# A router's matmuls turned round: weights stationary, all tokens moving, and the logits transposed back inside the next block

## The chip, the cores and the metric

The kernel runs on one core of a Trainium2 chip. The metric is the device time of one execution in microseconds, as the median of several runs; the kernel before takes 953.7 us.

## The reference

The input is x, 384 tokens by 1024 features, fp32. The first layer is graph attention (layer norm, q, k, v projections and their second projections, 16 heads, a mask built from 6144 edges, an output projection, added to x). The second is switch attention, and the change lies in its first step:

```python
def _get_sel_gate(x, w, route_scale):
    logits = jnp.einsum('bsd,ed->bse', x, w).astype(jnp.float32)
    raw = logits.reshape(x.shape[0], x.shape[1], H, E)
    probs = jax.nn.sigmoid(raw)
    vals, idx = jax.lax.top_k(probs, K)
    vals = vals / jnp.clip(vals.sum(-1, keepdims=True), 1e-09)
    vals = vals * route_scale
    gate = (jax.nn.one_hot(idx, E, dtype=vals.dtype) * vals[..., None]).sum(-2)
    return gate
gate_v = _get_sel_gate(x, sel_v_w, rs)
gate_o = _get_sel_gate(x, sel_o_w, rs)
```

Here x is the layer-normed sum after the first layer, H = 8 heads, E = 8 experts, K = 2. The 64 + 64 rows of sel_v_w and sel_o_w are one block of 128 router outputs. The gates weigh the experts' values and outputs of each head (v = sum over experts of gate_v times x @ v_w; out = sum of gate_o times context @ o_w), between which lies ordinary attention with q and k.

## The kernel before, in words

Weights come from HBM as 201 units of 128 x 1024 fp32 (512 KB), through a ring of three slots. SyncE issues a load for a slot once its low part is made (line 247). ScalarE copies the unit to fp32r, the high part (`hi_fixed`, lines 340 to 345, and `hi_at`, 330 to 338), after the unit two earlier has been used. GpSimd subtracts (`make_lo`, line 277) and gives the low part. TensorE then works a unit with three matmuls for each product, high by high, high by low, low by high (`three`, lines 994 to 998).

Two sorts of unit matter. In a column unit (`column_unit`, lines 1005 to 1011) a 128 x 128 block of the weights is stationary and the 384 tokens of the transposed activations hT move: 8 steps of three matmuls of 384 columns; the result has outputs on the partitions and tokens along the row. In a row unit (`row_unit`) a block of activations is stationary and 512 columns of weights move.

Between the two layers the order is this. The last output projection finishes token tile after token tile (t = 0, 1, 2). VectorE adds each to x (line 793) and makes its statistics; GpSimd makes 1/sqrt (lines 269, 272); ScalarE normalises into `normed` (line 350); TensorE transposes 8 blocks (`normed_turns`, lines 1045 to 1055, by `turn`, line 1043); ScalarE copies each half to hT_hi (`hT_his`, line 357); VectorE subtracts to hT_lo (`hT_los`, line 595).

The router (lines 1160 to 1177) is the unit U_ROUTER. Before the change it has the activations stationary and 128 columns of weights moving, for each tile by itself: 24 matmuls of 128 columns for tile 0, then the transposes of tile 2, then 24 for tile 1 and 24 for tile 2. Its result has tokens on the partitions, as the gates need it. When all are done, ScalarE takes the exponential of the logits (line 464), and VectorE runs a chain of small instructions, each waiting for the one before (lines 822 to 858): sigmoid, two largest of eight, their weights, the gates (line 857). ScalarE's order by hand is: normalise 0, normalise 1, hT_his 0, normalise 2, hT_his 1, weight copy U_ROUTER + 1, hT_his 2, weight copy U_ROUTER + 2, the exponential, further weight copies.

On TensorE the router is followed by head 0's q unit (U_HEAD, bank 5) and k unit, three of the four value units of the first four experts, three transposes of the gates (which wait for `gates_ready`), the fourth value unit, the scores, and from there the heads' loop without a change. The value units begin only after `router_exp`, since they write bank 2, which holds the logits. `normed` and the start of the logits' new place (`logits_T`) are the same piece of `scratch`, columns 3072 on; it is free once tile 0's transposes are done.

Of the kernel before, what the change touches and what calls it, by code (L numbers as in the profile page):

```python
# [14 lines left out]
P = 128  # L15
N = 384
NT = N // P
D = 1024
KT = D // P
# [13 lines left out]
RING = 3  # L33
U_PAIR = 3 * PAIRS
U_WO = U_PAIR + 3 * PAIRS
U_ROUTER = U_WO + 8
U_HEAD = U_ROUTER + 1
# [9 lines left out]
LN_STEPS = 2 * NT  # L47
RF = 2
GF = 7
QF, KF = 5, 0  # L50
# [33 lines left out]
def gnn_switch_kernel(nc, x_in, units, biases, bo, edge_type_weights, route_scale, edge_cols, src_row, dst_row, out):  # L84
    fp32, f32r, bf16 = mybir.dt.float32, mybir.dt.float32r, mybir.dt.bfloat16
    fp16, int32 = mybir.dt.float16, mybir.dt.int32
    ALU, ACT, AX = mybir.AluOpType, mybir.ActivationFunctionType, mybir.AxisListType.X

    ctx = ExitStack()
    with ctx:  # L90
        def sb(name, shape, dt):
            return ctx.enter_context(nc.sbuf_tensor(name, shape, dt))

        def sem(name):
            return ctx.enter_context(nc.semaphore(name))
# [3 lines left out]
        w_hi = sb("w_hi", [P, RING, D], f32r)  # L99
        w_lo = sb("w_lo", [P, RING, D], f32r)  # L100

        hT_hi, hT_lo = sb("hT_hi", [P, KT, N], f32r), sb("hT_lo", [P, KT, N], f32r)
# [14 lines left out]
        scratch = sb("scratch", [P, 6144], fp32)  # L117
# [47 lines left out]
        bank = [ctx.enter_context(nc.psum_tensor(f"bank{i}", [P, 512], fp32)) for i in range(8)]  # L165
# [6 lines left out]
        hi_ready, unit_used = sem("hi_ready"), sem("unit_used")  # L172
        lo_ready = [sem(f"lo_ready{s}") for s in range(RING)]
# [5 lines left out]
        normed_T, hT_hi_done, hT_lo_done = sem("normed_T"), sem("hT_hi_done"), sem("hT_lo_done")  # L179
# [23 lines left out]
        v_gated, fv_hi_done, fv_lo_done = sem("v_gated"), sem("fv_hi_done"), sem("fv_lo_done")  # L203
        f_scores, f_max, f_exp, f_norm = sem("f_scores"), sem("f_max"), sem("f_exp"), sem("f_norm")
        f_probs_T, f_pT_hi, f_pT_lo = sem("f_probs_T"), sem("f_pT_hi"), sem("f_pT_lo")
        f_context, context_ready = sem("f_context"), sem("context_ready")
        gated_ready, gc_hi_done, gc_lo_done, out_added = (sem("gated_ready"), sem("gc_hi_done"), sem("gc_lo_done"),
                                                          sem("out_added"))
# [1 line left out]


        bo_row = mask8[:].rearrange("p t n -> p (t n)")[:, 0:D]

        x_tiles = x_in.rearrange("(t p) d -> p t d", p=P)
        out_tiles = out.rearrange("(t p) d -> p t d", p=P)
# [106 lines left out]
        def _(act):  # L322
# [17 lines left out]
            def hi_fixed(u, fresh=False):  # L340
                s = u % RING
                act.wait_ge(raw_landed[s], 16 * (u // RING + 1))
                if not fresh:
                    act.wait_ge(unit_used, u - (RING - 1))
                act.activation(w_hi[:, s, :], w_raw[:, s, :], ACT.Copy).then_inc(hi_ready, 1)

            def normalise(turn, t):

                act.wait_ge(rstd_ready, turn * NT + t + 1)
                act.activation(normed[:, t, :], x[:, t, :], ACT.Identity, scale=rstd[:, t:t + 1],  # L350
                               bias=shift[:, t:t + 1]).then_inc(normed_ready, 1)

            def hT_his(turn, t):
                for f in range(2):
                    n = 2 * t + f
                    act.wait_ge(normed_T, turn * LN_STEPS + n + 1)
                    act.activation(hT_hi[:, 4 * f:4 * f + 4, t * P:(t + 1) * P],
                                   bank[LN_BANKS[n]][:].rearrange("p (k n) -> p k n", k=4),
                                   ACT.Copy).then_inc(hT_hi_done, 1)
# [93 lines left out]
            for u in range(U_WO + 5, U_ROUTER + 1):  # L453
# [3 lines left out]
            hT_his(1, 0)  # L457
            normalise(1, 2)
            hT_his(1, 1)
            hi_fixed(U_ROUTER + 1)  # L460
            hT_his(1, 2)
            hi_fixed(U_ROUTER + 2)
            act.wait_ge(unit_used, U_ROUTER + 1)
            act.activation(route[:, 0].rearrange("p g e -> p (g e)"), bank[RF][:, 0:N], ACT.Exp,
                           scale=-1.0).then_inc(router_exp, 1)

# [526 lines left out]
        def _(pe):  # L993
            def three(dst, a_hi, a_lo, b_hi, b_lo, first, last):

                pe.matmul(dst, a_hi, b_hi, start=first, stop=False)  # L996
                pe.matmul(dst, a_hi, b_lo, start=False, stop=False)  # L997
                return pe.matmul(dst, a_lo, b_hi, start=False, stop=last)  # L998

            def unit_ready(turns, u):  # L1000

                pe.wait_ge(lo_ready[u % RING], turns + (u // RING + 1))
                return u % RING

            def column_unit(turns, u, dst, b_hi, b_lo):
                s = unit_ready(turns, u)
                for k in range(KT):
                    c = slice(k * P, (k + 1) * P)
                    last = three(dst[:, 0:N], w_hi[:, s, c], w_lo[:, s, c], b_hi[:, k, :], b_lo[:, k, :], k == 0,
                                 k == KT - 1)  # L1010
                last.then_inc(unit_used, 1)
# [30 lines left out]
            def turn(dst, src):  # L1042
                return pe.transpose(dst, src, ident[:])  # L1043

            def normed_turns(turns, t):
                if turns == 0 and t == NT - 1:
                    pe.wait_ge(last_normed, 1)
                else:
                    pe.wait_ge(normed_ready, turns * (NT - 1) + t + 1)
                for f in range(2):  # L1050
                    n = 2 * t + f
                    for kk in range(4):
                        k = 4 * f + kk
                        last = turn(bank[LN_BANKS[n]][:, kk * P:(kk + 1) * P], normed[:, t, k * P:(k + 1) * P])
                    last.then_inc(normed_T, 1)
# [7 lines left out]
            for i in range(3):  # L1063
                column_unit(0, i, bank[i], hT_hi, hT_lo)
            with pe.Fori(1, PAIRS) as j:
                for i in range(3):
                    pe.wait_ge(qkv_lo_done, j * 3 + (i - 2))
                    column_unit(j, i, bank[i], hT_hi, hT_lo)
# [40 lines left out]

            pe.wait_ge(qkv_lo_done, PAIRS * 3 - 2)  # L1110
            column_unit(0, U_PAIR, bank[6], qT_hi, qT_lo)
            pe.wait_ge(qkv_lo_done, PAIRS * 3 - 1)
            column_unit(0, U_PAIR + 1, bank[0], kT_hi, kT_lo)
# [34 lines left out]
            for t in range(NT):  # L1148
                tok = slice(t * P, (t + 1) * P)
                for k in range(4, KT):  # L1150
                    s = s_7 if k > 5 else s_6
                    c = slice(k % 2 * HALF, (k % 2 + 1) * HALF)
                    last = three(bank[WO_BANKS[1][t]][:, 0:HALF], oT_hi[:, k, tok], oT_lo[:, k, tok], w_hi[:, s, c],
                                 w_lo[:, s, c], False, k == KT - 1)
# [2 lines left out]
                last.then_inc(unit_used if t == NT - 1 else tile_done, 1)  # L1157


            def router(t):  # L1160
                pe.wait_ge(hT_lo_done, LN_STEPS + 2 * t + 2)
                tok = slice(t * P, (t + 1) * P)
                for k in range(KT):
                    c = slice(k * P, (k + 1) * P)
                    s = U_ROUTER % RING
                    last = three(bank[RF][:, tok], hT_hi[:, k, tok], hT_lo[:, k, tok], w_hi[:, s, c], w_lo[:, s, c],
                                 k == 0, k == KT - 1)
                return last

            normed_turns(1, 0)  # L1170
            normed_turns(1, 1)
            pe.wait_ge(lo_ready[U_ROUTER % RING], U_ROUTER // RING + 1)
            pe.wait_ge(out_added, 2 * NT)
            router(0)
            normed_turns(1, 2)
            router(1)
            router(2).then_inc(unit_used, 1)


            def values_units(head, g, turns, u, experts=range(4), third=None):  # L1180
# [33 lines left out]
                    row_unit(turns, u + i, OF[f], gc_hi, gc_lo, i,  # L1214
                             (out_added, head * 6 + 7) if f else None)

            column_unit(0, U_HEAD, bank[QF], hT_hi, hT_lo)
            column_unit(0, U_HEAD + 1, bank[KF], hT_hi, hT_lo)
            pe.wait_ge(router_exp, 1)
            values_units(0, 0, 0, U_HEAD + 2, range(3))  # L1220
# [1 line left out]
            for t in range(NT):  # L1222
                last = turn(bank[GF][0:FH * FE, t * P:(t + 1) * P], gates[:, t, FH * FE:2 * FH * FE])
# [40 lines left out]
            for n in range(8):  # L1264
                f, i = n // 4, n % 4
                u = U_LAST + n
# [68 lines left out]
```

## Time and profile before

| | |
|---|---|
| median of 3 runs | 953.7 us (953.54 to 954.23) |
| the profiled execution | 953.67 us |
| its span, first to last instruction | 951.9 us |
| TensorE matmul busy | 934.1 us |
| VectorE, ScalarE, GpSimd busy | 484.0, 370.9, 512.9 us |
| HBM traffic | 130 MB, 137 GB/s over the span |

The span is 1.8 us shorter than the execution's own time, for what lies around the instructions. Busy times of TensorE are overlaps of pipelined matmuls, so the distance from start to start tells a matmul's price, not its duration. "PE" in the rows is TensorE, "DVE" VectorE, "ACT" ScalarE, "POOL" GpSimd. Times in the rows are us from the start of the span.

### The profile page before, as it was taken

What the parts mean: (1) busy time and instruction counts of PE and PEld (TensorE: products, weight loads), DVE (VectorE), ACT (ScalarE), POOL (GpSimd) and SP (SyncE); (2) the same over time, 40 slices, a digit from 0 to 9 for tenths busy, and PEclk for the clock granted to TensorE, in tenths of its full rate; (3) what the DMA queues carried; (4) which work ended last, traced back from release to release, by engine and by line L of the source; (5) the groups of instructions that cost most, each with busy time, mean ns of one, the idle gap of its engine ahead of it and who ended that gap; (6) DMA issues with size and microseconds to landing.
All of it is one profiled execution on the core that took longest, in us unless ns stands there. A gap on an engine that the chain in (4) does not pass through costs nothing.

```text
span 951.9 us, 14149 instructions
## 1 busy us (share of the span) xinstructions
PE 934.1 (98%) x4779; PEld 830.4 (87%) x4779; DVE 484.0 (51%) x1065; ACT 370.9 (39%) x593; POOL 512.9 (54%) x265
## 2 busy tenths in 40 slices
PE   5999999999999999999999999999999999999998
PEld 4999999999988879888888888888888888888887
DVE  7988855565652683812731642362182264154361
ACT  4333355455642423423433332343243243243331
POOL 4677763434335455565555555565556546556553
PEclk9999999999999999999999999999999999999999
DMA  7656643221223245443443353354353335335332
GB/s 277 183 187 185 183 134 105 75 86 66 88 82 104 80 136 178 177 133 113 149 158 132 103 198 118 132 174 134 117 184 118 132 120 185 113 111 199 133 111 89
DMA packets 38134, 130.43 MB, mean 137 GB/s; under 512 B 5920, under 2 KB 7648, under 8 KB 37088
## 3 DMA queue, kind: packets, MB, share of 16 engines
q1 hardware_dynamic: 31632, 110.25, 34.0%
q10 hardware_dynamic: 4944, 19.86, 6.5%
q0 software_dynamic: 1536, 0.03, 0.1%
q8 instruction: 14, 0.23, 0.1%
q14 instruction: 8, 0.07, 0.0%
HBM read 127.83 MB, written 2.29 MB: 137 GB/s over the span
## 4 chain that ended last, share of the span: by engine, by line
PE 83%; DMA 5%; DVE 4%; issue 4%; POOL 3%; ACT 1%; POOLq 0%; SPq 0%; DVEq 0%; ACTq 0%
PE bank L996 26%; PE bank L998 26%; PE bank L997 26%; DMA mask_scratch<-weight,cell 3%; POOL mask_scratch L281 3%; PE bank L1043 3%; PE bank L1080 1%; DMA x<-in_x 1%; DVE scratch L650 1%; DMA mask<-mask_scratch 0%; DVE scratch L832 0%; DVE scratch L836 0%; ACT scratch L417 0%; DVE scratch L855 0%; DVE scratch L825 0%
## 5 line engine op out<-in xcount | busy, mean ns | idle before, releaser
L277 POOL TENSOR_TENSOR w_lo<-w_raw,w_hi 128x1024 fp32r<-128x1024 f32 x184 | 449.4, 2446 | 388.8 <-ACT w_hi L338 317.6
L338 ACT ACTIVATE w_hi<-w_raw 128x1024 fp32r<-128x1024 f32 x166 | 175.5, 1058 | 211.4 <-PE bank L998 210.8
L996 PE MATMUL bank<-w_hi,hT_hi 128*128 128x512 f32 (+1 forms) x456 | 175.0, 384 | 0.8 <-DVE hT_lo L595 0.8
L998 PE MATMUL bank<-w_hi,hT_lo 128*128 128x512 f32 (+1 forms) x456 | 175.1, 384 | 0.0
L997 PE MATMUL bank<-w_lo,hT_hi 128*128 128x512 f32 (+1 forms) x456 | 175.0, 384 | 0.0
L996 PE MATMUL bank<-w_hi,qT_hi 128*128 128x512 f32 x384 | 150.1, 391 | 0.0
L998 PE MATMUL bank<-w_hi,qT_lo 128*128 128x512 f32 x384 | 149.5, 389 | 0.0
L997 PE MATMUL bank<-w_lo,qT_hi 128*128 128x512 f32 x384 | 149.4, 389 | 0.0
L934 DVE TENSOR_TENSOR x<-bank,x 128x512 f32<-128x512 f32 x48 | 30.4, 684 | 184.4 <-PE bank L998 184.4
L996 PE MATMUL bank<-hT_hi,w_hi 128*128 128x384 f32 x320 | 107.8, 337 | 1.5 <-DVE hT_lo L595 1.5
L997 PE MATMUL bank<-hT_lo,w_hi 128*128 128x384 f32 x320 | 107.5, 336 | 0.0
L998 PE MATMUL bank<-hT_hi,w_lo 128*128 128x384 f32 x320 | 107.5, 336 | 0.0
L996 PEld LDWEIGHTS bank<-w_hi,hT_hi 128*128 128x128 f32 x456 | 85.7, 188 | 17.4 <-issue 1.0
L998 PEld LDWEIGHTS bank<-w_hi,hT_lo 128*128 128x128 f32 x456 | 85.7, 188 | 17.0
L997 PEld LDWEIGHTS bank<-w_lo,hT_hi 128*128 128x128 f32 x456 | 85.7, 188 | 16.4
L880 DVE SCALAR_TENSOR_TENSOR scratch<-bank,v_gate,scratch 128x128 f32<-128x128 f32 x168 | 53.1, 348 | 80.7 <-PE bank L998 77.4
L998 PEld LDWEIGHTS bank<-w_hi,qT_lo 128*128 128x128 f32 x384 | 72.1, 188 | 15.1
L997 PEld LDWEIGHTS bank<-w_lo,qT_hi 128*128 128x128 f32 x384 | 72.1, 188 | 14.8
L996 PEld LDWEIGHTS bank<-w_hi,qT_hi 128*128 128x128 f32 x384 | 72.1, 188 | 14.6
L919 DVE TENSOR_TENSOR scratch<-scratch 128x384 f32<-128x384 f32 x64 | 63.8, 1006 | 16.4 <-ACT scratch L489 14.7
L281 POOL DMA_INDIRECT mask_scratch<-weight,cell x48 | 54.7, 1141 | 26.0 <-issue 13.8
L996 PEld LDWEIGHTS bank<-hT_hi,w_hi 128*128 128x128 f32 x320 | 60.6, 189 | 2.1 <-DVE hT_lo L595 1.9
(155 smaller groups left out, 1278.0 us busy)
## 6 DMA issues: line engine op xcount, KB each, us to landing
w_raw<-in_units SPq DMA_DIRECT2D x201, 512.0 KB, 3.3
scratch<-gate_rows_scratch ACTq DMA_DIRECT2D x8, 1536.0 KB, 7.3
scratch<-in_src_row ACTq DMA_DIRECT2D x8, 384.0 KB, 4.2
scratch<-in_dst_row ACTq DMA_DIRECT2D x8, 384.0 KB, 5.3
out_x<-x SPq DMA_DIRECT2D x6, 256.0 KB, 2.1
x<-in_x SPq DMA_DIRECT2D x2, 512.0 KB, 6.8
mask_scratch<-weight,cell POOLq DMA_INDIRECT x48
mask<-mask_scratch ACTq DMA_DIRECT2D x1, 576.0 KB, 3.9
```

Source lines behind the costliest of these rows:

```text
L277: pool.tensor_tensor(w_lo[:, s, :], w_raw[:, s, :], w_hi[:, s, :].bitcast(fp32), ALU.subtract).then_inc(lo_ready[s], 1)
L281: pool.indirect_dma_start(out=mask_dram, out_offset=bass.IndirectOffsetOnAxis(ap=cells, axis=0), in_=values, in_offset=None, bounds_check= ...
L338: act.activation(w_hi[:, s, :], w_raw[:, s, :], ACT.Copy).then_inc(hi_ready, 1)
L650: step.add(dve.scalar_tensor_tensor(same[:, start:start + wide], keys[:, c * P:PIECE * P], key[:, bass.ds(at, 1)], later[:, 0:wide], ALU.i ...
L880: ins = dve.scalar_tensor_tensor(v_sum[:, t, :], src, col, v_sum[:, t, :], ALU.mult, ALU.add)
L919: dve.tensor_tensor(gated[:, e % 2, :], context, gate_rows[:, e, :], ALU.mult).then_inc(gated_ready, 1)
L934: dve.tensor_tensor(x[:, t, f * HALF:(f + 1) * HALF], bank[banks[t]][:, 0:HALF], x[:, t, f * HALF:(f + 1) * HALF], ALU.add).then_inc(out_a ...
L996: pe.matmul(dst, a_hi, b_hi, start=first, stop=False)
L997: pe.matmul(dst, a_hi, b_lo, start=False, stop=False)
L998: return pe.matmul(dst, a_lo, b_hi, start=False, stop=last)
L1043: return pe.transpose(dst, src, ident[:])
L1080: last = pe.matmul(bank[NT * head + t][:, 0:N], a[p, tok], b[p, :], start=n == 0, stop=n == 2)
```

## The change

Four things: the router becomes one column unit with its weights stationary and all 384 tokens moving, after all three tiles are transposed and split; ScalarE copies its result from bank 2 to SBUF; three transposes turn it back into bank 2, and they stand on TensorE after the second of eight steps of head 0's q unit; and ScalarE makes hT_his of tile 2 before the weight copy U_ROUTER + 1, not after. The exponential waits for the transposes.

```diff
@@ declarations
+        logits_ready, logits_back = sem("logits_ready"), sem("logits_back")
+        logits_T = scratch[:, 3072:3072 + N]
@@ ScalarE
             normalise(1, 2)
             hT_his(1, 1)
+            hT_his(1, 2)
             hi_fixed(U_ROUTER + 1)
-            hT_his(1, 2)
             hi_fixed(U_ROUTER + 2)
             act.wait_ge(unit_used, U_ROUTER + 1)
+            act.activation(logits_T, bank[RF][:, 0:N], ACT.Copy).then_inc(logits_ready, 1)
+            act.wait_ge(logits_back, 1)
             act.activation(route[:, 0].rearrange("p g e -> p (g e)"), bank[RF][:, 0:N], ACT.Exp,
                            scale=-1.0).then_inc(router_exp, 1)
@@ TensorE
-            def column_unit(turns, u, dst, b_hi, b_lo):
+            def column_unit(turns, u, dst, b_hi, b_lo, between=None):
                 s = unit_ready(turns, u)
                 for k in range(KT):
+                    if between and k == 2:
+                        between()
                     c = slice(k * P, (k + 1) * P)
                     last = three(dst[:, 0:N], w_hi[:, s, c], w_lo[:, s, c], b_hi[:, k, :], b_lo[:, k, :], k == 0,
                                  k == KT - 1)
@@ TensorE
-            def router(t):
-                pe.wait_ge(hT_lo_done, LN_STEPS + 2 * t + 2)
-                tok = slice(t * P, (t + 1) * P)
-                for k in range(KT):
-                    c = slice(k * P, (k + 1) * P)
-                    s = U_ROUTER % RING
-                    last = three(bank[RF][:, tok], hT_hi[:, k, tok], hT_lo[:, k, tok], w_hi[:, s, c], w_lo[:, s, c],
-                                 k == 0, k == KT - 1)
-                return last
-
-            normed_turns(1, 0)
-            normed_turns(1, 1)
-            pe.wait_ge(lo_ready[U_ROUTER % RING], U_ROUTER // RING + 1)
-            pe.wait_ge(out_added, 2 * NT)
-            router(0)
-            normed_turns(1, 2)
-            router(1)
-            router(2).then_inc(unit_used, 1)
+            def router():
+                pe.wait_ge(hT_lo_done, 2 * LN_STEPS)
+                pe.wait_ge(out_added, 2 * NT)
+                column_unit(0, U_ROUTER, bank[RF], hT_hi, hT_lo)
+
+            def logit_turns():
+                pe.wait_ge(logits_ready, 1)
+                for t in range(NT):
+                    last = turn(bank[RF][:, t * P:(t + 1) * P], logits_T[:, t * P:(t + 1) * P])
+                last.then_inc(logits_back, 1)
+
+            for t in range(NT):
+                normed_turns(1, t)
+            router()
@@ TensorE
-            column_unit(0, U_HEAD, bank[QF], hT_hi, hT_lo)
+            column_unit(0, U_HEAD, bank[QF], hT_hi, hT_lo, logit_turns)
```

## Rows read from the trace of the kernel before

**Rows 1.** The page: busy time of each engine, and the chain by engine.
```profile
PE 934.1 (98%) x4779; PEld 830.4 (87%) x4779; DVE 484.0 (51%) x1065; ACT 370.9 (39%) x593; POOL 512.9 (54%) x265
PE 83%; DMA 5%; DVE 4%; issue 4%; POOL 3%; ACT 1%; POOLq 0%; SPq 0%; DVEq 0%; ACTq 0%
```

**Rows 2.** Groups by line, TensorE's matmuls, 315.1 to 324.07: busy, mean ns, idle before.
```profile
L996 PE MATMUL bank<-w_hi,hT_hi 128*128 128x128 f32 x24 | 6.6, 277 | 0.8 <-DVE hT_lo L595 0.8
```

**Rows 3.** Timeline of TensorE: start, duration, idle before and what ended it.
```profile
311.66 1.04 PE L1043 MATMUL bank<-ident,scratch 128*128 128x128 f32 x8
...
315.17 0.30 PE L996 MATMUL bank<-w_hi,hT_hi 128*128 128x128 f32 x1 [0.80 <-DVE hT_lo L595]
...
317.87 1.06 PE L1043 MATMUL bank<-ident,scratch 128*128 128x128 f32 x8
318.69 0.30 PE L996 MATMUL bank<-w_hi,hT_hi 128*128 128x128 f32 x1
...
323.97 0.28 PE L998 MATMUL bank<-w_hi,hT_lo 128*128 128x128 f32 x1
324.08 0.39 PE L996 MATMUL bank<-hT_hi,w_hi 128*128 128x384 f32 x1
...
328.31 0.33 PE L996 MATMUL bank<-hT_hi,w_hi 128*128 128x384 f32 x1
...
344.53 0.39 PE L998 MATMUL bank<-w_hi,hT_lo 128*128 128x512 f32 x1
345.75 0.52 PE L1043 MATMUL bank<-ident,mask 128*64 128x128 f32 x3 [0.84 <-DVE mask L857]
```

**Rows 4.** Timeline of ScalarE around the router.
```profile
314.70 1.24 ACT L350 ACTIVATE scratch<-x,shift,rstd 128x1024 f32<-128x1024 f32 x1 [0.51 <-POOL shift L272]
...
316.80 1.06 ACT L345 ACTIVATE w_hi<-w_raw 128x1024 fp32r<-128x1024 f32 x1
318.53 1.09 ACT L357 ACTIVATE hT_hi<-bank 128x512 fp32r<-128x512 f32 x2 [0.67 <-PE bank L1043]
...
324.28 0.49 ACT L464 ACTIVATE scratch<-bank 128x384 f32<-128x384 f32 x1 [3.72 <-PE bank L998]
...
328.57 1.06 ACT L345 ACTIVATE w_hi<-w_raw 128x1024 fp32r<-128x1024 f32 x1 [2.85 <-PE bank L998]
```

**Rows 5.** Timeline of VectorE: the splits of hT, and three of the gates' chain.
```profile
313.74 1.29 DVE L595 TENSOR_TENSOR hT_lo<-bank,hT_hi 128x512 fp32r<-128x512 f32 x2
316.46 1.29 DVE L595 TENSOR_TENSOR hT_lo<-bank,hT_hi 128x512 fp32r<-128x512 f32 x2 [1.44 <-ACT hT_hi L357]
319.16 1.29 DVE L595 TENSOR_TENSOR hT_lo<-bank,hT_hi 128x512 fp32r<-128x512 f32 x2 [1.42 <-ACT hT_hi L357]
...
341.21 0.21 DVE L849 TENSOR_TENSOR best<-best 128x48 f32<-128x48 f32 x1
...
342.36 2.75 DVE L855 TENSOR_TENSOR scratch<-scratch,best 128x384 f32<-128x384 f32 x1
345.14 0.56 DVE L857 TENSOR_TENSOR mask<-scratch 128x384 f32<-128x384 f32 x1
```

**Rows 6.** Timeline of GpSimd: two of its weight subtractions.
```profile
342.07 2.62 POOL L277 TENSOR_TENSOR w_lo<-w_raw,w_hi 128x1024 fp32r<-128x1024 f32 x1 [1.67 <-ACT w_hi L345]
346.15 2.40 POOL L277 TENSOR_TENSOR w_lo<-w_raw,w_hi 128x1024 fp32r<-128x1024 f32 x1 [1.46 <-ACT w_hi L345]
```

**Rows 7.** Timeline of TensorE at the start.
```profile
12.09 3.68 PE L1043 MATMUL bank<-ident,scratch 128*128 128x128 f32 x16 [0.64 <-ACT scratch L350]
17.23 0.69 PE L996 MATMUL bank<-hT_hi,w_hi 128*128 128x384 f32 x1 [1.46 <-DVE hT_lo L595]
...
20.23 0.33 PE L996 MATMUL bank<-hT_hi,w_hi 128*128 128x384 f32 x1
```

**Rows 8.** Windows, start-up: length, busy of PE, PEld, DVE, ACT, POOL, clock, DMA, GB/s.
```profile
10.00:20.00 10.00, 7.90 (x32) 7.10 (x31) 8.66 (x15) 8.60 (x12) 5.42 (x6) 1.00 0.90 322
```

## The prediction, made before the changed kernel was run

> **What bounds the kernel now.** I read the page first. TensorE is busy in 98% of the span and holds 83% of the chain that ended last [rows 1], so a change pays only where it shortens TensorE's own stream or a wait in it. Then the groups of TensorE's instructions in the router's stretch: 72 matmuls and 8 transposes fill 8.9 us (315.17 to 324.08), 24 of each of three kinds as in the row, with a wait of 0.8 us ahead of them [rows 2, 3]. The matmuls move 128 columns and start 0.111 us apart: (323.97 - 318.69) / 47 = 0.112. The next block, head 0's q with 384 columns moving, takes 24 matmuls from 324.08 to 328.31, 4.23 us, or 0.176 each [rows 3]. So the same arithmetic costs about half with the weights stationary.
>
> Then TensorE's order of time after the router: it has issued all it may at 344.76 (344.53 and the 0.23 by which 512-column matmuls follow each other) and begins again at 345.75, released by VectorE's line 857, the last of the gates [rows 3]. This wait decides the case. What sets the end at 345.75 is a chain and not TensorE: router ends, ScalarE's exponential at 324.28 [rows 4], VectorE's top-two work to the end of line 857 at 345.70 (345.14 + 0.56) [rows 5]. TensorE has 1.0 us to spare against it. Afterwards TensorE runs without a wait to the end of the span, so the change is worth what line 857 is moved by, and no more.
>
> **The sum, part by part.**
>
> (1) *When all tokens are ready.* The router now starts once, after tile 2's last hT_lo. ScalarE's normalise of tile 2 is not moved: 314.70 + 1.24 = 315.94 [rows 4]. Its transposes no longer stand behind the first router tile, so they start at about 316.0, not 317.87. Four of them let ScalarE copy after 318.53 - 317.87 = 0.66 us, at 316.65. ScalarE is busy with tile 1's copies until 316.80, the moment at which it now takes the weight copy; the moved hT copies take that place: 316.80, not 318.53. VectorE starts its subtraction 0.63 us after ScalarE (319.16 - 318.53), which would be 317.43, but tile 1's pair holds it until 316.46 + 1.29 = 317.75. The pair ends at 319.04 [rows 5]. TensorE followed such a pair by 0.14 (315.17 - (313.74 + 1.29)) [rows 3, 5]. Router start: **319.18**, 4.0 us later than now.
>
> (2) *The router.* 24 matmuls as in head 0's q: 4.23 us, end of issue 323.41, against 324.08: 0.67 us earlier. Half the work is gone (8.0 us of matmuls become 4.2), but most of that goes into waiting for tile 2.
>
> (3) *The way back.* The exponential now starts 0.31 us after the last router matmul starts (324.28 - 323.97), that matmul being 0.28 long; with one of 0.33 ScalarE's copy starts at 323.24 + 0.33 + 0.04 = 323.61. Its length is that of the exponential of the same shape, 0.49 [rows 4]: 324.10. TensorE meanwhile has six matmuls of head 0's q, 6 x 0.176 = 1.06 us, until 324.47; they cover the copy with 0.4 us to spare, and without them TensorE would stand for the 0.7 us itself. The transposes' spacing is that of the eight between 317.87 and 318.69, 0.10 to 0.11 [rows 3]: three are 0.33 us. The last starts at about 324.7, ends 0.28 later, and the exponential starts at **325.05**, 0.77 us later than 324.28.
>
> (4) *VectorE's chain.* At its present length it would end at 345.70 + 0.77 = 346.47. But its length depends on GpSimd. Line 855 takes 2.75 us (342.36 to 345.11), line 857, with the same shapes, 0.56 [rows 5]; line 855 ends 0.42 after GpSimd's subtraction of 342.07 + 2.62 = 344.69 [rows 6]. Four instructions of the chain with both inputs in SBUF are held so (2.3 to 2.8 us each). GpSimd's schedule follows TensorE's blocks, which move by -0.67 + 0.33 = -0.34 us, while VectorE moves by +0.77. I replayed the chain with the rule that whichever of the two starts first holds the other; with today's times it gives 345.68. With the shifts the last hold falls on line 849 (now 341.21, between two subtractions): GpSimd's instruction runs 341.73 to 344.13, and then lines 849 to 857 follow unhindered, 0.06 + 0.27 + 3 x 0.56 with gaps, 2.1 us: 346.25. **Line 857 ends 0.5 us later.** If the shifts differ by 0.1 less, the replay passes through another order and gives 0.05; with no help from the holds it is 0.8. These are the ends.
>
> (5) *TensorE's side.* It would reach the gates' transposes at 344.76 - 0.34 = 344.4, so its wait grows from 1.0 us to 1.8. The 4 us of matmuls saved are gone: 3.4 of them waiting for tile 2, the rest in this wait.
>
> (6) *What is moved on other queues.* On ScalarE the weight copy of head 0's q goes behind the two hT copies: 317.9 instead of 316.80; GpSimd's part then runs 319.1 to 321.5, needed at 323.41: 1.9 us of cover. The next weight copy ends by 320.1, its GpSimd part by 323.9, needed at 328.0. The load into the first slot starts 1.1 us later and has until 328 (ScalarE's copy at 328.57 [rows 4]), over 6 us. ScalarE now also stands at the wait for the transposes; behind it is the weight copy for the first values block, which moves from 324.67 to 325.4, its GpSimd part ready near 329.0 and needed at 332.2. All free; without the 1.9 us of cover a slip would go into the router's end one for one.
>
> Sum: +0.5 us for everything behind the gates. The profiled execution took 953.67 us (its span 951.9 and 1.8 around it), so 954.17; it stands 0.03 under the median of 953.70, and I forecast **954.2 us**. A measurement of this kernel can tell about 0.2%, 1.9 us, from no change; this is inside it.
>
> **Clock.** In the start-up stretch transposes ran from 12.09 for 3.68 us, 0.23 us each, and the ten matmuls from 17.23 to 20.23 still started 0.33 us apart on the mean: 384 columns in that time are the level of 1.2 GHz, and the 0.176 later that of 2.4 [rows 3, 7]. The granted clock of that stretch nevertheless reads 1.00 [rows 8], so I go by spacing. Around the router the spacing shows no fall now: TensorE has transposes and two short waits from 311.66 to 315.17, 3.5 us, and then starts fast [rows 3]. With the change the stretch without matmuls lasts until 319.18, 7.5 us, with 24 transposes (some 2.7 us) in it.
> The Trainium skill, TensorE: Matmul & The Clock Gate, "What's actually happening", lets the clock fall to 1.2 GHz after idleness, and "Part 4: PE-mode transpose" says that transposes do not count as busy in the same way. By these the router would start slow and the sum would be rival A's. The trace agrees in so far as transposes did not lift the clock at the start [rows 7]; it shows no fall.
>
> **Rivals.**
>
> *A, slower: the clock falls before the router.* Place: the 7.5 us just named; it decides if transposes do not keep the clock up. Price: at the start the nine spacings from 17.23 to 20.23 took 3.00 us, where 9 x 0.176 are 1.58: 1.4 us lost before the clock rose. If all 24 router matmuls ran slow, 24 x (0.32 - 0.176) = 3.5 us. It falls fully on the gates' chain. I take 2.1, nearer the only rise that is seen: 956.3 (955.6 to 957.7). For it: a stretch twice the present one, and the start-up transposes. Against: the present 3.5 us without matmuls did nothing, and the stretch is not idle.
>
> *B, slower: one more hold.* Line 857 starts now at 345.14, GpSimd's next subtraction at 346.15 [rows 5, 6]. If that one comes first, line 857 is held for its 2.4 us: 956.6. The replay puts line 857 ahead, though in (4) by only 0.1 us, and behind once the shifts of the two differ by 1.6 us and not 1.1. The Trainium skill, SBUF — State Buffer, "Who interferes with whom", gives the port to the one that starts first, for its whole instruction; the row at 342.36 agrees.
>
> *C, faster: the gates' chain gives way.* Had it no weight at all, TensorE could gain its present wait of 1.0 us and the 0.3 of (5): 1.3 us: 952.4. That is still inside 0.2%. Only an error in several terms at once makes it faster by more.
>
> *D, the change does not do what it says:* the router's matmuls do not get their 0.176 because their weights are freshly made and start late. Then it ends by up to 1 us later: 955.2, inside the bound too.
>
> **The numbers.** Forecast 0.50, its own range 953.3 to 955.2 (the ends of (4) and a few tenths between executions, with D above); C 0.03 and D 0.05, both inside the bound; A 0.35, of which 0.02 falls under the bound; B 0.05; faster by several errors at once 0.02. So same 0.50 + 0.03 + 0.05 + 0.02 = 0.60, slower by over 0.2% (above 955.6) 0.33 + 0.05 = 0.38, faster (below 951.8) 0.02. The range 953.3 to 957.1 leaves out the top of A and a little below, under 2 in 10.
>
> **What would show it.** Right: router matmuls from about 319.2, 0.174 apart; the copy near 323.6; three transposes after the sixth matmul of head 0's q with no gap; the exponential near 325.0; the wait at line 857 grown to about 1.8 us; everything after it shifted by 0.5. Wrong: router matmuls 0.32 apart (A), a 2.4 us line 857 (B), a gap inside head 0's q, or a wait at the gates under 1 us.

## The result and the profile after

The changed kernel takes 955.79 us in the median of 22 runs (953.97 to 957.42), the kernel before 954.12 us in 22 runs of its own. The ratio is 1.0016, 95% interval 1.0008 to 1.0023: about 1.5 us slower, inside the 0.2% that I had called no change. The profiled execution took 955.83 us, its span 954.1.

The page of the changed kernel, busy time of each engine, beside [rows 1]:

```profile
PE 932.1 (98%) x4734; PEld 828.0 (87%) x4734; DVE 483.9 (51%) x1065; ACT 371.6 (39%) x594; POOL 512.5 (54%) x265
```

TensorE does 2 us less and the end comes later. Its timeline around the router answers to [rows 3]:

```profile
310.93 1.04 PE L1050 MATMUL bank<-ident,scratch 128*128 128x128 f32 x8
312.55 1.09 PE L1050 MATMUL bank<-ident,scratch 128*128 128x128 f32 x8 [0.58 <-ACT scratch L353]
315.27 1.09 PE L1050 MATMUL bank<-ident,scratch 128*128 128x128 f32 x8 [1.62 <-ACT scratch L353]
318.27 0.69 PE L1001 MATMUL bank<-hT_hi,w_hi 128*128 128x384 f32 x1 [1.91 <-DVE hT_lo L600]
318.75 0.53 PE L1002 MATMUL bank<-hT_lo,w_hi 128*128 128x384 f32 x1
319.07 0.53 PE L1003 MATMUL bank<-hT_hi,w_lo 128*128 128x384 f32 x1
...
324.08 0.34 PE L1001 MATMUL bank<-hT_hi,w_hi 128*128 128x384 f32 x1
324.25 0.34 PE L1002 MATMUL bank<-hT_lo,w_hi 128*128 128x384 f32 x1
...
326.17 0.49 PE L1050 MATMUL bank<-ident,scratch 128*128 128x128 f32 x3
...
347.98 0.52 PE L1050 MATMUL bank<-ident,mask 128*64 128x128 f32 x3 [1.75 <-DVE mask L862]
```

The router's matmuls start 0.32 us apart until 324, then 0.17. So until 324 TensorE is at the lower level. Here the granted clock shows it too. Windows of the changed kernel: length, busy of PE, PEld, DVE, ACT, POOL, clock, DMA, GB/s:

```profile
316.00:317.00 1.00, 0.36 (x4) 0.12 (x2) 1.00 (x3) 1.00 (x3) 0.00 (x0) 1.00 0.07 16
317.00:318.00 1.00, 0.00 (x0) 0.00 (x0) 1.00 (x3) 1.00 (x3) 0.00 (x0) 0.54 0.00 0
318.00:323.00 5.00, 4.73 (x15) 4.73 (x16) 0.21 (x1) 1.05 (x2) 4.70 (x2) 0.50 0.20 68
323.00:324.00 1.00, 1.00 (x5) 1.00 (x4) 0.00 (x0) 0.00 (x0) 0.00 (x0) 0.55 0.46 184
324.00:325.00 1.00, 1.00 (x8) 1.00 (x7) 0.00 (x0) 0.00 (x0) 0.00 (x0) 1.00 0.99 283
```

It falls to one half, 1.2 GHz, just after 317, in the wait for hT_lo ahead of the router, and is back at 324. So this execution is rival A of the prediction.

ScalarE has the copy and the exponential [rows 4]:

```profile
325.32 0.49 ACT L467 ACTIVATE scratch<-bank 128x384 f32<-128x384 f32 x1 [6.27 <-PE bank L1003]
326.69 0.49 ACT L469 ACTIVATE scratch<-bank 128x384 f32<-128x384 f32 x1 [0.88 <-PE bank L1050]
```

**A measure for the stretch.** In the traces of this case this part begins between 310.2 and 313.1 us, so I do not compare clock times of two traces but the distance from the first transposes of tile 0 (row 310.93 here, 311.66 in [rows 3]) to the transposes of the gates, which end TensorE's wait. Before: 345.75 - 311.66 = 34.09 us. Changed: 347.98 - 310.93 = 37.05 us, 2.96 more. Below it is called the stretch. What follows it is the same in every trace that has the gates' transposes in this place: the execution's time less 347.98, the end of the stretch, is 607.85 us in the changed kernel, 607.92 before, and between 607.79 and 608.14 in all ten such traces. So the kernels differ in the stretch alone, and a good part of the spread between executions of one kernel comes from when the stretch begins.

### The profile page after: what moved, and what is told of

Read it like the earlier page. It is cut to its first block, busy times and chain, and to the rows that moved or that the text cites. A ratio compares the mean times of both kernels' runs of the same rounds, so it can differ in the third digit from the quotient of the medians.

```text
span 954.1 us, 14060 instructions
## 1 busy us (share of the span) xinstructions
PE 932.1 (98%) x4734; PEld 828.0 (87%) x4734; DVE 483.9 (51%) x1065; ACT 371.6 (39%) x594; POOL 512.5 (54%) x265
## 4 chain that ended last, share of the span: by engine, by line
PE 83%; DVE 4%; DMA 4%; issue 4%; POOL 4%; ACT 1%; POOLq 0%; SPq 0%; DVEq 0%; ACTq 0%
PE bank L1001 26%; PE bank L1003 26%; PE bank L1002 26%; DMA mask_scratch<-weight,cell 3%; POOL mask_scratch L284 3%; PE bank L1050 3%; PE bank L1087 1%; DVE scratch L655 1%; DMA x<-in_x 1%; DMA mask<-mask_scratch 0%; DVE scratch L837 0%; DVE scratch L844 0%; ACT scratch L420 0%; DVE scratch L841 0%; DVE stats L586 0%
## 5 line engine op out<-in xcount | busy, mean ns | idle before, releaser
L1003 PE MATMUL bank<-w_hi,hT_lo 128*128 128x512 f32 x432 | 168.5, 390 | 0.0
L1002 PE MATMUL bank<-w_lo,hT_hi 128*128 128x512 f32 x432 | 168.4, 390 | 0.0
L1001 PE MATMUL bank<-w_hi,hT_hi 128*128 128x512 f32 x432 | 168.3, 390 | 0.0
L1001 PE MATMUL bank<-hT_hi,w_hi 128*128 128x384 f32 x328 | 111.2, 339 | 3.4 <-DVE hT_lo L600 3.4
L1002 PE MATMUL bank<-hT_lo,w_hi 128*128 128x384 f32 x328 | 110.7, 338 | 0.0
L1003 PE MATMUL bank<-hT_hi,w_lo 128*128 128x384 f32 x328 | 110.6, 337 | 0.0
L1003 PEld LDWEIGHTS bank<-w_hi,hT_lo 128*128 128x128 f32 x432 | 81.1, 188 | 17.0
L1002 PEld LDWEIGHTS bank<-w_lo,hT_hi 128*128 128x128 f32 x432 | 81.1, 188 | 16.4
L1001 PEld LDWEIGHTS bank<-w_hi,hT_hi 128*128 128x128 f32 x432 | 81.1, 188 | 16.3
```

## The experiments

All were timed against the kernel before on the same chip: e1 to e4 on one, e5 to e8 on a second, e9 to e12 on a third. Mean granted clocks are of single executions; one without a recorded fall reads 1.00. The fall of 3.4 us in e9's trace makes it 0.998, that of nearly 7 us in the changed kernel's 0.996.

**e1, unread matmuls in the idle time.**

```diff
-            for t in range(NT):
-                normed_turns(1, t)
+            def fill(n):
+                for _ in range(n):
+                    pe.matmul(bank[1][:, 0:N], k2_hi[:, 0:P], q2_hi[:], start=True, stop=True)
+
+            normed_turns(1, 0)
+            normed_turns(1, 1)
+            pe.wait_ge(out_added, 2 * NT)
+            fill(8)
+            normed_turns(1, 2)
+            fill(9)
             router()
```

> The changed kernel with 8 matmuls that nothing reads (384 columns, bank 1) between the transposes of tile 1 and tile 2 and 9 more between those of tile 2 and the router, in time in which TensorE stood. Theory (the stretch without matmuls lets the clock fall, and that is the loss): granted clock 1.00 throughout, router matmuls 0.17 to 0.18 us apart, the exponential 2.5 to 3 us earlier against the last projection matmul than in the changed kernel, time 0.3 to 0.8 us above the kernel before. Rival (the loss is the wait for tile 2 and the way back, the clock only goes along): time as the changed kernel, 1.5 to 2 us above the kernel before.

Measured: ratio 0.9996 (0.9985 to 1.0007), granted clock 1.00 in all of 12 executions. TensorE's timeline:

```profile
311.65 1.04 PE L1050 MATMUL bank<-ident,scratch 128*128 128x128 f32 x8
...
314.11 1.64 PE L1180 MATMUL bank<-q_hi,k_hi 128*128 128x384 f32 x8
315.99 1.09 PE L1050 MATMUL bank<-ident,scratch 128*128 128x128 f32 x8 [0.24 <-ACT scratch L353]
316.84 1.84 PE L1180 MATMUL bank<-q_hi,k_hi 128*128 128x384 f32 x9
318.99 0.45 PE L1001 MATMUL bank<-hT_hi,w_hi 128*128 128x384 f32 x1 [0.31 <-DVE hT_lo L600]
...
324.32 0.49 PE L1050 MATMUL bank<-ident,scratch 128*128 128x128 f32 x3
346.13 0.52 PE L1050 MATMUL bank<-ident,mask 128*64 128x128 f32 x3 [1.75 <-DVE mask L862]
```

Adding 17 matmuls that nothing reads makes the changed kernel faster: its ratio goes from 1.0016 to 0.9996. The stretch is 346.13 - 311.65 = 34.48 us: 2.57 under the changed kernel and 0.39 over the kernel before. So in these traces the fall costs 2.57 us, and everything else that the change does costs 0.39. The time expected, 0.3 to 0.8 us above the kernel before, did not show in the median, which is 0.4 below by the ratio; e9 gives the reason.

**e2, transposes in place of these matmuls** (12 and 14 of `pe.transpose(bank[1][:, 0:P], ident[:], ident[:])`).

> The changed kernel with 12 and 14 transposes of 128 columns in the same two places, in place of matmuls. If only matmuls keep the clock up: it falls to 0.50 near 317 in the profiled execution or in most of the others, time 1.5 to 2.5 us above the kernel before. If any work of TensorE keeps it up (it is idleness that lets it fall): clock 1.00, time 0.3 to 0.8 us above.

Measured: ratio 0.9994 (0.9983 to 1.0006), 11 of 12 executions at 1.00; the stretch is 344.74 - 310.28 = 34.46 us, as in e1. These transposes keep the clock up as the matmuls do.

```profile
312.83 1.47 PE L1180 MATMUL bank<-ident 128*128 128x128 f32 x12
314.62 1.09 PE L1050 MATMUL bank<-ident,scratch 128*128 128x128 f32 x8 [0.32 <-ACT scratch L353]
315.55 1.69 PE L1180 MATMUL bank<-ident 128*128 128x128 f32 x14
317.62 0.45 PE L1001 MATMUL bank<-hT_hi,w_hi 128*128 128x384 f32 x1 [0.38 <-DVE hT_lo L600]
```

From 311.9 to 317.6 there are only transposes here, and the router still starts at the upper level. What let the clock fall in the changed kernel was the idle time between, not the kind of work.

**e3, e1 without the way back.** It leaves out the turning of the logits, so its gates are others. The cuts against e1:

```diff
-            act.activation(logits_T, bank[RF][:, 0:N], ACT.Copy).then_inc(logits_ready, 1)
-            act.wait_ge(logits_back, 1)
...
-            column_unit(0, U_HEAD, bank[QF], hT_hi, hT_lo, logit_turns)
+            column_unit(0, U_HEAD, bank[QF], hT_hi, hT_lo)
```

> As e1, but without ScalarE's copy and the three transposes; the exponential reads the router's result as it is, outputs on the partitions. It leaves out the turning of the logits, so the gates are others. My sum prices the way back at 1.44 us of the exponential's start (0.49 copy, 0.4 standing behind q's matmuls, 0.33 transposes and latencies). Theory: exponential 1.4 us earlier than in e1, and line 862 earlier by 0.5 to 1.9 as the holds by GpSimd fall; time 0.2 to 0.8 us below the kernel before, since TensorE then waits less at the gates. If the way back is hidden: as e1.

Measured: ratio 0.9980 (0.9967 to 0.9992), 1.9 us less, where 0.2 to 0.8 was expected. The exponential, first in e1, then in e3:

```profile
324.85 0.49 ACT L469 ACTIVATE scratch<-bank 128x384 f32<-128x384 f32 x1 [0.88 <-PE bank L1050]
...
324.02 0.49 ACT L467 ACTIVATE scratch<-bank 128x384 f32<-128x384 f32 x1 [3.69 <-PE bank L1001]
```

In e1 the exponential starts 324.85 - 311.65 = 13.20 us into the stretch, here 324.02 - 312.21 = 11.81, 1.39 earlier (1.44 expected). The stretch is 345.43 - 312.21 = 33.22 us, 1.26 under e1. The way back lies on the gates' chain nearly whole, though inside q TensorE does not wait for it.

**e4, the router in two parts.** Weights stationary in both; `router()` is left with the tokens of tile 2; `router_part` works the unit for the tokens that it is given.

```diff
...
+            unit_ready(0, U_ROUTER)
+            pe.wait_ge(out_added, 2 * NT)
+            pe.wait_ge(hT_lo_done, LN_STEPS + 4)
+            router_part(slice(0, 2 * P))
             router()
```

> The changed kernel with the router in two parts, weights stationary in both: the 256 tokens of tiles 0 and 1 as soon as they are split, then the 128 of tile 2. 48 matmuls, not 24. The stretch without matmuls ends near 317 on the scale of the changed kernel, 1.3 us earlier. If the clock theory holds: clock 1.00 in most executions, router ends at 322.5 to 322.9 (24 x 0.12 and 24 x 0.112), as in e1 within 0.4 us; time 0.3 to 1 us above the kernel before. If the fall does not depend on the stretch's length: router slow, time 2.5 us or more above.

Measured: ratio 1.0001 (0.9990 to 1.0013), but only 4 of 12 executions at 1.00. Windows of its profiled execution:

```profile
317.00:318.00 1.00, 0.39 (x4) 0.15 (x2) 1.00 (x3) 1.00 (x3) 0.00 (x0) 0.91 0.00 0
318.00:319.00 1.00, 0.81 (x4) 0.84 (x5) 1.00 (x3) 1.00 (x2) 0.00 (x0) 0.50 0.00 0
...
321.00:322.00 1.00, 1.00 (x9) 1.00 (x9) 0.00 (x0) 0.00 (x0) 1.00 (x2) 0.88 0.00 0
```

The clock falls just before 318 and is back after 321; in the changed kernel it was away for twice as long. The stretch is 348.02 - 311.96 = 36.06 us. Half of my expectation failed (8 of 12 executions read under 1.00), and the time is within its interval of the one expected. The wait ahead of the router is 0.80 us here, not 1.91, and no execution reads 0.996: a shorter gap gave shorter falls, not none.

**e5, the gates later.** On the kernel before, the transposes of the gates go behind the fourth values unit, and the wait for their copy guards only the score tile that needs the bank.

```diff
+            values_units(0, 0, 0, U_HEAD + 2, (3,))
             pe.wait_ge(gates_ready, 1)
...
-            values_units(0, 0, 0, U_HEAD + 2, (3,))
-            pe.wait_ge(gateT_ready, 1)
-            f_scores_of(0)
+            f_scores_of(0, True)
...
+                    if first and t == NT - 1:
+                        pe.wait_ge(gateT_ready, 1)
```

> The kernel before with the three transposes of the gates moved behind the fourth values unit, and the wait for their copy moved from before the scores to before the third score tile (whose bank it guards). Theory (TensorE's wait at the gates is what ties everything to VectorE's chain, 1.0 us in the kernel before): that wait goes, nothing takes its place, time 0.8 to 1.0 us below the kernel before. Rival (the wait turns up again at the scores or at the second values group): no change.

Measured: ratio 0.9986 (0.9974 to 0.9997), about 1.3 us less. TensorE's waits no longer list line 857. From the start of the stretch to the end of the execution it takes 952.50 - 311.64 = 640.86 us, the kernel before 953.67 - 311.66 = 642.01: 1.15 less, for 0.8 to 1.0 expected. The chain of the gates was the bound, as the prediction had it.

**e6, e1 with the later gates.**

> e1 (changed kernel with the 17 unread matmuls) with the move of e5. Theory: TensorE's wait of 1.75 us at the gates goes; then TensorE's own stream counts, which is 0.3 us shorter than before: time 1.2 to 1.6 us below the kernel before, granted clock 1.00. Rival: the later gates are waited for at the scores, time as e1.

Measured: ratio 0.9967 (0.9955 to 0.9979), 3.1 us less, in 6 runs, more than the 1.2 to 1.6 expected. From the start of the stretch to the end it takes 951.86 - 311.51 = 640.35 us, 1.66 under the 642.01 of before. The medians differ by more in part because the kernel before has falls too (e9); how far that explains it was not separated. TensorE's waits of e6 (us in total, times, longest), without one for line 862:

```profile
PE bank L1050 <- ACT scratch L353: 10.8, 4, 8.4
PE bank L1001 <- DVE hT_lo L600: 1.8, 2, 1.5
PE bank L1050 <- DVE scratch L749: 0.6, 1, 0.6
```

**e7, e6 with tile 0 of the router in place of the second fill**, then tiles 1 and 2 together.

> e6, but the router is worked for tile 0 (128 columns, 24 matmuls) behind the transposes of tile 2, where e6 has 9 unread matmuls, and then for tiles 1 and 2 together (256 columns); weights stationary in both. Expected: 24 x 0.112 = 2.7 us from about 316.9, then 24 x 0.13 = 3.1 at most to 322.7, against 323.4 in e6: 0.5 to 0.9 us below e6, clock 1.00. If the 256 columns start late (tile 2 is split at 319.05, the first part ends at 319.6) or the two parts cost more, as e6.

Measured: ratio 0.9965 (0.9953 to 0.9977), in 6 runs. To the gates' transposes its distance is 346.04 - 310.19 = 35.85 us against 348.17 - 311.51 = 36.66 in e6 (where these stand one unit later than in the others): 0.81 less, as expected. The runs do not separate the two; both beat both kernels by about 3 us or more.

**e8, the kernel before with 4 unread matmuls** ahead of `router(0)`.

> The kernel before with 4 unread matmuls of 384 columns ahead of its first router tile, in the 0.8 us in which TensorE stood there. Half of the executions of the kernel before show a granted clock of 0.998, not 1.00. If that is a fall in this stretch through the thin activity before the router: all or nearly all at 1.00 and the median 0.3 to 0.8 us lower. If it comes from the router's own 128-column matmuls or from elsewhere: clocks as in the kernel before, no change.

Measured: ratio 0.9988 (0.9979 to 0.9997), 1.1 us less (0.3 to 0.8 expected), 10 of 12 executions at 1.00, against 10 of 23 of the kernel before on that chip. The stretch is 346.23 - 312.21 = 34.02 us, as in [rows 3]: the fill itself costs nothing.

**e9, the kernel before again.**

> The kernel before itself, for a second trace and a control. Half of its executions read a granted clock of 0.998 or less, against 2 in 36 of e1, e2 and e3. If that is a fall around the router also here, executions at 1.00 are about 1 us shorter on the median than those at 0.998, and e10 shows more and longer falls on the same chip. The ratio must be 1.000 within 0.001.

Measured: ratio 1.0004 (0.9993 to 1.0016); 10 of its 12 executions read 0.998 or 0.996. Its profiled execution (mean clock 0.998) has the fall that [rows 3] do not show:

```profile
317.00:318.00 1.00, 1.00 (x11) 1.00 (x11) 0.85 (x2) 1.00 (x3) 0.00 (x0) 1.00 0.00 0
318.00:319.00 1.00, 1.00 (x9) 1.00 (x9) 0.43 (x1) 0.55 (x1) 0.38 (x1) 0.76 0.00 0
319.00:320.00 1.00, 1.00 (x7) 1.00 (x6) 0.00 (x0) 0.30 (x1) 1.00 (x1) 0.50 0.00 0
...
322.00:323.00 1.00, 1.00 (x11) 1.00 (x11) 0.00 (x0) 0.10 (x1) 0.82 (x1) 1.00 0.80 229
```

The stretch is 348.07 - 312.34 = 35.73 us, 1.64 over that of [rows 3]. Of the 35 other executions of the kernel before on this chip 18 read 1.00 (median 952.75 us) and 17 read 0.998 (954.46 us). So the medians that e1, e2 and e3 are measured against hold such falls, which is why these came out lower than expected. Not each 0.998 need be a fall here: in the profiled executions of e5 and e11 the only one lies between 18 and 22, in the start-up.

**e10, the changed kernel again.**

> The changed kernel itself, beside e9, e11 and e12 on one chip. Expected: nearly all executions at 0.998 or 0.996, ratio 1.001 to 1.002.

Measured: ratio 1.0013 (1.0003 to 1.0023); 10 of 11 executions at 0.996 or 0.995. The stretch is 350.16 - 313.14 = 37.02 us, as in the first trace. This trace has a fall in the start-up too, so its mean reads 0.995.

**e11, the changed kernel with the later gates, no fill.**

> The changed kernel with the move of e5 and e6 but without unread matmuls. Theory: TensorE's wait at the gates, 1.8 us, goes, the fall of the clock stays: 1.5 to 1.8 us under e10 and 1.8 to 2.6 us above e6, so about at the kernel before. If the fall cost nothing once the gates are off the path, it would come to e6, 3 us below the kernel before.

Measured: ratio 0.9996 (0.9985 to 1.0007). It is 2.1 us under e10 (953.46 to 955.53), and its ratio is 0.0029, 2.8 us, above that of e6. Both differences are a little over what I expected (1.5 to 1.8 and 1.8 to 2.6), and the second one is between two chips. The two losses, clock and wait at the gates, stand side by side; taking one away leaves the other. But its profiled execution (mean clock 0.998, from the start-up) has the waits of the changed kernel and no fall behind them:

```profile
317.07 1.07 PE L1050 MATMUL bank<-ident,scratch 128*128 128x128 f32 x8 [1.72 <-ACT scratch L353]
319.98 0.44 PE L1001 MATMUL bank<-hT_hi,w_hi 128*128 128x384 f32 x1 [1.84 <-DVE hT_lo L600]
320.26 0.34 PE L1002 MATMUL bank<-hT_lo,w_hi 128*128 128x384 f32 x1
...
325.29 0.49 PE L1050 MATMUL bank<-ident,scratch 128*128 128x128 f32 x3
```

From the start of the stretch to the gates' transposes it takes 349.27 - 312.64 = 36.63 us, as e6 does with its fill (36.66). So this idle time lets the clock fall often, not always. Of the 12 executions the six at 0.996 or 0.995 have a median of 954.3 us, the two at 1.00 take 951.7 and 951.9.

**e12, e1 with the second fill alone.**

> e1 with only the 9 matmuls behind tile 2's transposes; the 1.6 us before these transposes stay idle, so the stretch without matmuls ends near 316.8 on the scale of the kernel before, not at 319.2. If the length of the stretch decides: few or no falls and the time of e1. If every idle gap in it counts by itself: falls in some executions, 0.5 to 1.5 us above e1.

Measured: ratio 0.9998 (0.9989 to 1.0006), 9 of 12 at 1.00, 2 at 0.999, 1 at 0.998; the stretch is 345.03 - 310.53 = 34.50 us. Filling the one of the two gaps that lies just ahead of the router is nearly enough.

## Why the prediction was right or wrong

**The range and the class held, the likeliest case did not.** I forecast 954.2, between 953.3 and 957.1, and no measurable change with 0.60. The ratio gives 1.5 us more and 955.79 lies in the range. But the way there is rival A's, to which I gave 0.35: the lower clock is in both profiled executions of the changed kernel, and of its 33 timed executions 25 read 0.996 or less and six 0.998.

That "no measurable change" came out is in part luck. The stretch grew by 2.96 us in the traces, 0.31% of the time, which is over the 0.2%; it is mainly because the kernel before loses time to the same effect in about half of its executions that the medians came closer. In the sum itself the step that failed is that TensorE starts the router at the upper level after its waits: the sum has 4.23 us for the router, and in the changed kernel it took 325.13 - 318.27 = 6.86, in e1 4.29. That is the 2.57 us. The rest of the sum, 0.5 us, held within about 0.1.

**Steps (1) and (2).** The router starts 318.27 - 310.93 = 7.34 us into the stretch, where I had 319.18 - 311.66 = 7.52; in e1 it is 7.34 too. In e1 the router takes 4.29 us to q's first matmul, for 4.23, and the copy starts 323.48 - 311.65 = 11.83 in, against 323.61 - 311.66 = 11.95. Right within 0.2 us. "Most of that goes into waiting for tile 2" is what the rows show: waits of 1.62 and 1.91 us where there was one of 0.8.

**Step (3).** The exponential was predicted 0.77 us later; measured in e1 it is 13.20 - 12.62 = 0.58 later (12.62 is 324.28 - 311.66). The cover by six matmuls held: no row of TensorE inside q waits.

**Step (4).** The chain was to give back about 0.2 to 0.3 of this, with the last hold on line 849. The instructions of the chain that are held in e1 (line 854 is the former 849):

```profile
329.54 2.65 DVE L837 TENSOR_TENSOR scratch<-scratch,desc 128x384 f32<-128x384 f32 x1
333.40 2.74 DVE L844 SCALAR_TENSOR_TENSOR scratch<-scratch 128x384 f32<-128x384 f32 x1
338.54 2.05 DVE L841 TENSOR_TENSOR scratch<-scratch,best 128x384 f32<-128x384 f32 x1
341.58 2.42 DVE L854 TENSOR_TENSOR best<-best 128x48 f32<-128x48 f32 x1
```

In part other instructions are held than before ([rows 5] show line 855), and the last is the one named. The chain gave back 0.58 - 0.39 = 0.19 us, and the stretch grows by 0.39, for 0.5 predicted. Rival B did not come: line 862 takes 0.56 us in e1.

**Step (5).** TensorE's wait at the gates was to grow from 1.0 to 1.8 us. The profile's own figures are 0.84 before [rows 3] and 1.75 in the changed kernel and in e1, a growth of 0.91 for 0.8. Of it 0.39 is the chain, and 0.52 is that TensorE is done earlier, where the prediction had 0.34.

**Rival A: the event right, its condition wrong, its price short.** I wrote that it "decides if transposes do not keep the clock up". e2 refutes that: they do. The start-up rows misled me. In [rows 7] the transposes did not lift the clock, but that is one execution. The same 16 take 2.71 us in e11 and 3.35 in e5, and in the changed kernel the first matmuls after them start 0.17 to 0.28 us apart. In e10 the clock rises while they run:

```profile
11.04 1.94 PE L1050 MATMUL bank<-ident,scratch 128*128 128x128 f32 x8 [11.04 <-ACT scratch L353]
13.31 2.97 PE L1050 MATMUL bank<-ident,scratch 128*128 128x128 f32 x16 [0.33 <-ACT scratch L353]
18.45 0.45 PE L1001 MATMUL bank<-hT_hi,w_hi 128*128 128x384 f32 x1 [2.17 <-DVE hT_lo L600]
18.73 0.43 PE L1002 MATMUL bank<-hT_lo,w_hi 128*128 128x384 f32 x1
18.96 0.53 PE L1003 MATMUL bank<-hT_hi,w_lo 128*128 128x384 f32 x1
```

Sixteen transposes take 2.97 us, not the 3.68 of [rows 7]; then an idle wait of 2.2 us, and from the third matmul on the spacing is that of the lower level again. So of what I took from the Trainium skill (TensorE: Matmul & The Clock Gate), the fall to 1.2 GHz after idleness ("What's actually happening") agrees with the windows above, where the clock falls in a wait. That transposes do not count as busy in the same way ("Part 4: PE-mode transpose") does not agree with e2, where 26 of them held the clock up in 11 of 12 executions, nor with e10's start-up. With idleness as the condition the present gaps could have been compared with the coming ones: 0.58 and 0.80 us against 0.58, 1.62 and 1.91. The price, 2.1 us, was measured as 2.57; about 18 of the router's 24 matmuls were slow, nearer to my upper bound (all 24, 3.5 us) than to the nine of the start-up (1.4 us).

**And the baseline.** My argument against A, that the present stretch "did nothing", rested on one trace. e9's trace and the clocks of e8 show that the kernel before has the fall in about half of its executions, at 1.64 us in the one trace that has it. That is why the median moved by 1.5 us and not by 3: 0.39 + 2.57 in most executions of the changed kernel, and less in those that read 0.998 (their median is 954.25 us in the first 22, against 955.88 of those at 0.996), set against about half of 1.64 in those of before. This gives at most 2.1, an estimate from single traces, inside the interval of 0.8 to 2.2 us.

## What to carry to other kernels

Halving TensorE's work in a block pays nothing if the block then waits for its last input and a chain on another engine sets the next wait. Here the gates' chain did, and moving the consumer of that chain one unit later was worth more than the change. Where a rearrangement opens idle time on TensorE just ahead of dense work, price the lower clock for that work, and look at the clock over many executions of both kernels, since one trace shows one draw. Work that nothing reads, put into such idle time, can be a gain: 17 matmuls took the loss away.

## What the runs showed of the hardware

Whether the clock falls differs between executions of the same program, and a fall is commoner with more idle time ahead of the router: a mean clock under 1.00 in none of 12 in e1, 2 of 12 in e8, 17 of 35, 13 of 23, 17 of 35 and 10 of 12 of the kernel before, 10 of 12 in e11, 10 of 11 in e10. These shares are upper bounds, since a fall in the start-up lowers the mean too. A fall comes in the idle wait or some time after it: in e9 it begins at about 318.5 with TensorE busy since 315.9. In the start-up [rows 7, 8] the granted clock reads 1.00 where the spacing is 0.32 us, the spacing that goes with 0.50 in the changed kernel; so ahead of the first recorded change the reading can be wrong. What decides whether the clock falls in one execution and not in another (e10 and e11, with the same waits to 0.1 us) stays open. Why the lower level lasts some 3 us in one execution and nearly 7 in another was not tried.
